# Value biases written into PSUM by ScalarE, low parts read from PSUM by VectorE, final normalisation on GpSimd

## The reference

```python
def layer(h, params):                      # second network, two layers
    u = einsum('bid,bjd->bij', h, h) / sqrt(D)
    a = softmax(u, axis=-1)
    delta = a * adjacency_matrix
    attn = delta / (sum(delta, axis=-1, keepdims=True) + 1e-10)
    hl = h @ wl.T + b_l
    hs = h @ ws.T + b_s
    hr = h @ wr.T + b_r
    ctx = (attn * upper) @ hl + diag(attn)[..., None] * hs + (attn * lower) @ hr
    o = (ctx - mean(ctx)) / sqrt(var(ctx) + 1e-12) * g + beta
    return relu(o)
...
x = layernorm(x + first_network(x, adj))
x = layernorm(x + second_network(x, adj))
```

## Time and profile before

| what | us |
|---|---|
| median of 3 runs | 1744.8 (1744.64 to 1747.77) |
| the profiled execution | 1744.34 |
| its span, first to last instruction | 1742.2 |
| TensorE busy | 1676.6 |
| VectorE, ScalarE, GpSimd busy | 1286.0, 884.4, 824.6 |
| TensorE's mean granted clock | 0.991 of full |

### The profile page before, as it was taken

One profiled execution on the slowest core, in us unless ns is written; L12 is line 12 of the kernel. 1 busy time (PEld: TensorE's weight loads), 2 busy tenths in 40 slices (PEclk: granted clock), 3 DMA queues, 4 the chain that ended last, 5 costly groups with the idle time before them and its releaser, 6 DMA issues.

```text
span 1742.2 us, 30190 instructions
## 1 busy us (share of the span) xinstructions
PE 1676.6 (96%) x9664; PEld 1581.4 (91%) x9664; DVE 1286.0 (74%) x2783; ACT 884.4 (51%) x1785; POOL 824.6 (47%) x860
## 2 busy tenths in 40 slices
PE   7999999999999999999999999999999999999994
PEld 6989989888988989989899999999999999999994
DVE  4587685967868587786877868678686786867866
ACT  4545455464554545455454545545455454544542
POOL 5143242423324243244466646567375663656635
PEclk9999999999999999999999999999999999999997
DMA  7015021020300202031131220303103021030201
GB/s 226 1 31 154 6 82 38 24 90 6 114 6 24 92 29 90 6 87 45 50 85 24 71 44 22 93 0 80 35 21 93 0 81 34 21 93 0 76 1 36
DMA packets 107991, 92.00 MB, mean 53 GB/s; under 512 B 63280, under 2 KB 101168, under 8 KB 107952
## 3 DMA queue, kind: packets, MB, share of 16 engines
q1 hardware_dynamic: 107952, 91.51, 18.3%
HBM read 66.33 MB, written 25.17 MB: 53 GB/s over the span
## 4 chain that ended last, share of the span: by engine, by line
issue 46%; POOL 27%; PE 19%; DVE 5%; ACT 2%; SPq 1%; POOLq 1%; DMA 0%; DVEq 0%; ACTq 0%
PE b_work L1153 11%; POOL s_v_lo L1347 8%; POOL g_qv_lo L622 3%; POOL b_ht L602 3%; POOL b_z L1371 3%; PE b_work L372 2%; POOL b_z L1373 2%; PE b_work L1165 2%; POOL s_expo L1358 1%; POOL s_keep L1341 1%; POOL s_rstd L1362 1%; PE b_score_ps L386 1%; PE b_work L396 1%; POOL g_keep_l L617 1%; POOL g_sigma L631 1%
## 5 line engine op out<-in xcount | busy, mean ns | idle before, releaser
L1153 PE MATMUL b_work<-b_w_hi,b_ht 128*128 128x384 f32 x2304 | 605.4, 337 | 2.4 <-DVE b_z L1500 1.7
L1153 PEld LDWEIGHTS b_work<-b_w_hi,b_ht 128*128 128x128 f32 x2304 | 418.0, 188 | 3.6 <-DVE b_z L1500 2.6
L1153 PE MATMUL b_work<-b_w_lo,b_ht 128*128 128x384 f32 x1152 | 385.3, 334 | 0.0
L372 PE MATMUL b_work<-b_ht,b_w_hi 128*128 128x512 f32 x1152 | 357.4, 391 | 9.8 <-DVE b_w_lo L697 9.8
L1347 POOL TENSOR_TENSOR s_v_lo<-s_v_full,s_v_hi 128x384 fp32r<-128x384 f32 x256 | 245.7, 978 | 197.4 <-ACT s_v_hi L1250 196.6
L622 POOL TENSOR_TENSOR g_qv_lo<-g_v_full,g_qv_hi 128x384 fp32r<-128x384 f32 x128 | 132.6, 1055 | 363.7 <-ACT g_qv_hi L495 363.7
L372 PEld LDWEIGHTS b_work<-b_ht,b_w_hi 128*128 128x128 f32 x1152 | 216.1, 189 | 51.4 <-issue 9.8
L372 PE MATMUL b_work<-b_ht,b_w_lo 128*128 128x512 f32 x576 | 225.8, 392 | 0.0
L1153 PEld LDWEIGHTS b_work<-b_w_lo,b_ht 128*128 128x128 f32 x1152 | 216.7, 188 | 0.0
L729 DVE TENSOR_TENSOR g_qv_lo<-b_work,g_qv_hi 128x512 fp32r<-128x512 f32 x192 | 128.7, 686 | 112.0 <-ACT g_qv_hi L483 110.2
L396 PE MATMUL b_work<-b_w_hi,b_ht 128*128 128x384 f32 x768 | 206.2, 336 | 0.0
(11 more groups left out here) (137 smaller groups left out, 3226.4 us busy)
## 6 DMA issues: line engine op xcount, KB each, us to landing
b_x_in<-in_x_t SPq DMA_DIRECT2D x16, 768.0 KB, 7.0
g_x_res<-in_x SPq DMA_DIRECT2D x16, 768.0 KB, 7.6
x<-b_z SPq DMA_DIRECT2D x16, 768.0 KB, 3.8
b_x_in<-x SPq DMA_DIRECT2D x64, 192.0 KB, 6.8
s_x_res<-x SPq DMA_DIRECT2D x16, 768.0 KB, 7.0
out<-b_z SPq DMA_DIRECT2D x15, 768.0 KB, 4.1
b_a_tr<-in_adj_t SPq DMA_DIRECT2D x64, 64.0 KB, 3.4
g_a_nat<-in_adj SPq DMA_DIRECT2D x32, 64.0 KB, 2.4
```

The lines of the kernel that those rows point to most:

```text
L372: mm = pe.matmul(bank[:], w, h, start=(n == 0), stop=(n == len(pairs) - 1))
L1153: mm = pe.matmul(bank[:, 0:H], h, w, start=(n == 0), stop=(n == len(pairs) - 1))
```

## The change

ScalarE writes ("seeds") the bias of a value job of side 0 or 1 into its bank before TensorE starts, and TensorE adds its nine products to it. ScalarE then copies the high part out of the bank, VectorE subtracts it from the bank and writes the low part, which frees the bank. `v_full` and GpSimd's `values_lo` are gone, and a value job of side 0 or 1 waits for its seed (`seeded`) in place of the free bank. The four final normalisations per unit move from ScalarE to GpSimd, except in the last pass. ScalarE's order within a unit is written anew; VectorE makes the probabilities ahead of jobs 3 to 5. At the hand-over VectorE's flips and low parts come earlier and the residual later, ScalarE's third `next_turn_out` comes earlier, two memsets move from GpSimd to VectorE, GpSimd's masks of stream 1 go ahead of its weight parts, and SyncE's first store goes ahead of two weight loads.

The diff, cut to its core:

```diff
@@ gated network, ScalarE, last unit
                     next_turn_out(0)
                     next_turn_out(1)
+                    next_turn_out(2)
                 exponentials(i, unit)
...
-                if not more:
-                    next_turn_out(2)
@@ gated network, VectorE, query parts of the last unit
                             query_lo(i, unit + 1, j)
+                            if last and unit == UNITS - 2 and j == QB - 2:
+                                next_flip(0)
+                                next_flip(1)
@@ gated network, VectorE, up_to_contexts
-                if s is not None:
+                if s is not None and more:
                     add_residual(i, s)
...
                 if not more:
-                    next_flip(0)
-                    next_flip(1)
-                mask_scores(i, unit)
-                if not more:
                     next_turn_lo(0)
                     next_flip(2)
+                    next_turn_lo(1)
+                    next_turn_lo(2)
+                mask_scores(i, unit)
                 biased_value(i, unit, 1)
...
                 biased_value(i, unit, 3, uses=1 if more else 2)
+                if not more:
+                    add_residual(i, s)
@@ SyncE
             sp.wait_ge(folded, 1)
+            store_last(0)
             load_weight(0)
             load_weight(1)
-            store_last(0)
@@ TensorE, values
-                bank = work_bank(i, unit, j)
+                if side < 2:
+                    pe.wait_ge(seeded, nth(i, unit, 2 * NT, 2 * t + side))
+                    bank = work[(unit * WN + j) % RING]
+                else:
+                    bank = work_bank(i, unit, j)
...
-                    mm = pe.matmul(bank[:, 0:H], h, w, start=(n == 0), stop=(n == len(pairs) - 1))
+                    mm = pe.matmul(bank[:, 0:H], h, w, start=(n == 0 and side == 2), stop=(n == len(pairs) - 1),
+                                   skip_group_check=True)
@@ TensorE, contexts
-                    pe.wait_ge(v_lo_ready, nth(i, unit, 2 * NT, 2 * t + 1))
+                    pe.wait_ge(work_free, freed(i, unit, t * SIDES + 1))
@@ ScalarE
-            def values_hi(i, unit, t):
...
+            def seed(i, unit, j):
+                t, side = value_job(j)
+                act.wait_ge(work_free, freed(i, unit, j - RING))
+                nc.scalar.activation(work[(unit * WN + j) % RING][:, 0:H], bias[:, side, layer_of(unit), :], ACT.Copy)\
+                    .then_inc(seeded, 1)
+
+            def value_hi(i, unit, j):
+                t, side = value_job(j)
+                act.wait_ge(work_full, nth(i, unit, WN, j))
+                nc.scalar.activation(v_hi[:, t, side, 0:H], work[(unit * WN + j) % RING][:, 0:H], ACT.Copy)\
+                    .then_inc(v_hi_ready, 1)
...
             def first_half(i, unit):
+                seed(i, unit, 0)
+                seed(i, unit, 1)
                 exponentials(i, unit)
-                values_hi(i, unit, 0)
+                seed(i, unit, 3)
+                value_hi(i, unit, 0)
+                value_hi(i, unit, 1)
+                seed(i, unit, 4)
             def second_half(i, unit, more, tail):
-                values_hi(i, unit, 1)
...
                 probabilities_hi(i, unit)
+                value_hi(i, unit, 6)
+                seed(i, unit, 9)
+                if flip_next:
+                    turn_out(i, unit + 1, 0)
+                value_hi(i, unit, 7)
+                seed(i, unit, 10)
+                if flip_next:
+                    turn_out(i, unit + 1, 1)
                 if tail:
                     gated_normalise(1)
-                flip_next = more and layer_of(unit + 1) == 0
-                if flip_next:
+                if turn_next:
                     turn_out(i, unit + 1, 0)
                     turn_out(i, unit + 1, 1)
-                values_hi(i, unit, 2)
+                value_hi(i, unit, 9)
                 if more:
-                    for k in range(2 if flip_next else 0, KO):
-                        turn_out(i, unit + 1, k)
-                values_hi(i, unit, 3)
+                    turn_out(i, unit + 1, 2)
+                value_hi(i, unit, 10)
@@ ScalarE, one_pass
                         first_half(i, unit + 1)
-                    normalise(i, unit, more)
-                    if more:
+                        seed(i, unit + 1, 6)
+                        normalise(i, unit, (0, 1))
+                        value_hi(i, unit + 1, 3)
+                        normalise(i, unit, (2, 3))
+                        value_hi(i, unit + 1, 4)
+                        seed(i, unit + 1, 7)
                         second_half(i, unit + 1, not (last and unit == UNITS - 2), first and unit == 0)
...
-                    if unit >= STREAMS:
+                    if last and unit >= STREAMS:
                         final_normalise(i, unit - STREAMS, tiles=NT if more else NT // 2)
@@ ScalarE, first unit: exponentials, seed 3, high parts of probabilities, then
+            value_hi(0, 0, 0)
+            value_hi(0, 0, 1)
+            seed(0, 0, 4)
+            seed(0, 0, 6)
             gated_normalise(0)
-            values_hi(0, 0, 0)
-            values_hi(0, 0, 1)
+            value_hi(0, 0, 3)
+            value_hi(0, 0, 4)
+            seed(0, 0, 7)
             weight_hi(0)
+            value_hi(0, 0, 6)
+            seed(0, 0, 9)
@@ GpSimd
+            def final_normalise(s):
+                for t in range(NT):
+                    nc.gpsimd.tensor_scalar(z[s][:, t, 0:H], z[s][:, t, 0:H], frstd[s][:, t:t + 1],
+                                            foffset[s][:, t:t + 1], ALU.mult, ALU.add).then_inc(out_ready, 1)
...
                     roots(i, unit)
-                    if more:
-                        values_lo(i, unit + 1, 0)
...
+                    if unit == 0 and not first:
+                        final_normalise(1)
+                    if unit == UNITS - 1 and not last:
+                        final_normalise(0)
@@ VectorE, biased_value
                 if side < 2:
...
+                    dve.wait_ge(v_hi_ready, nth(i, unit, 2 * NT, 2 * t + side))
+                    nc.vector.tensor_tensor(v_lo[:, t, side, 0:H], bank[:, 0:H], v_hi[:, t, side, 0:H].bitcast(F32),
+                                            ALU.subtract).then_inc(work_free, 1)
@@ VectorE, up_to_contexts
+                probabilities(i, unit)
                 for j in range(3, 6):
                     biased_value(i, unit, j)
...
-                probabilities(i, unit)
+                probabilities_lo(i, unit)
                 biased_value(i, unit, 6)
-                probabilities_lo(i, unit)
```

More of the change, by code:

```diff
@@ L949, in softmax_layers @@
     LAST_GT = 1
-    VF = 4
     HALF = P // 2
@@ L1257, in final_normalise, with normalise @@
                                          bias=foffset[s][:, t:t + 1]).then_inc(out_ready, 1)
-            def normalise(i, unit, more):
+            def normalise(i, unit, tiles):
                 layer, s = divmod(unit, STREAMS)
                 act.wait_ge(offset_ready, nth(i, unit, 1, 0))
-                for t in range(NT if layer == 0 or more else LAST_GT):
+                for t in tiles:
                     nc.scalar.activation(z[s][:, t, 0:H], z[s][:, t, 0:H], ACT.Identity, scale=rstd[:, t:t + 1],
@@ L1646, in _ @@
             nc.vector.memset(v_own[:, :, H:H + 1], 1.0)
+            nc.vector.memset(v_hi[:, :, :, H:HC].bitcast(F32), 1.0)
+            nc.vector.memset(v_lo[:, :, :, H:HC].bitcast(F32), 0.0)
             biased_value(0, 0, 3)
```

60 lines of the change are left out of this document (21 added, 39 removed).

## The result

The changed kernel takes 1732.74 us (median of 4 runs, 1731.75 to 1733.57) against 1745.92 us of the kernel before, run beside it: ratio 0.9919, 95% interval 0.9907 to 0.9931. Profiled execution to profiled execution it is 1731.75 against 1744.34 us, span 1730.2 against 1742.2: -12.0 us of span where the sum said -18.0. Faster, as forecast, and 5.7 us above the predicted 1727.

The account below looks back on a forecast made before the run. TensorE, busy for 96% of the span, was taken to bound the kernel. Terms -15.4 - 4.5 + 0.4 + 1.5 = -18.0 us against 1744.34 gave 1726.3, for the median 1727; range 1716 to 1738.

Parts of the forecast that it names:

- (1): Contexts of the unit after the fourth, seven passes: TensorE's paired waits on GpSimd's low parts go, -15.4 us.
- (2): TensorE's slow stretches that begin near those waits: with the waits gone the clock drops go, -4.5 us.
- (3): Middle of all units: ScalarE's added seeds and high-part copies from PSUM fit without delaying TensorE, 0 us.
- (4): At 14 unit boundaries: job 0 also waits for a seed, but VectorE comes earlier; net +0.4 us.
- (7): Tail behind the last matmul: it keeps its instructions, 0 us.
- (5): Final normalisation moved to GpSimd: about 1.0 us a tile, taken up by slack in its queue, 0 us.
- (6): Hand-over to the second network: earlier start, then waits on late seeds and weights; net +1.5 us.
- Late boundary: Unit boundaries: GpSimd's normalisation takes 1.96 us a tile, seven waits partly return, 9 us, 1736 us; chance 0.14.

Follow-up runs that it names:

- the kernel with the forty memsets: Changed kernel plus 40 one-column memsets in front of VectorE's program, their tile allocated behind all others: 1724.79 us, ratio 0.9884.

## Why the prediction was right, and where it was off

The direction was right, and the waits and slow stretches that were to go went. Two signs named for it did not come: passes take 106.65 us and not 105.9, and outside the first unit TensorE waits 1.04 to 1.20 us for a seed once per pass, where well under 0.3 was said. The median lies 0.7 us above the forecast's own band of 1722 to 1732.

(1) **The pairs.** Right, and mis-sized to the bad side. No wait on GpSimd is left in the contexts. But they cost more than the 15.4 us of the list. From the contexts' first matmul to the next fold that unit took 6.90 to 6.97 us in the passes without a clock drop, and takes 4.25 now: 2.7 us a pass, 18.8 in seven. In the kernel before, the last matmul ahead of the longer wait is this, and the next, the first of the earlier trace rows, starts 2.04 us after it where 0.18 is usual:

```profile
1198.29 0.34 PE L1165 MATMUL b_work<-s_v_hi,s_prob_lo 128*128 128x386 f32 x1
```

The list shows 1.71 us of that.

(2) **The clock.** Right. The passes at 0.98 are at 1.00, and no TensorE wait of 1.7 us stands ahead of them: 109.73 + 109.68 + 109.45 less three times 108.1 is -4.6 us, against -4.5. The new wait of 1.04 to 1.20 us leaves the clock at 1.00.

(3) **The middle of a unit.** Right, nearly to the figure. Lines by cost, changed kernel (busy, mean ns | idle before):

```profile
L1492 DVE TENSOR_TENSOR s_v_lo<-b_work,s_v_hi 128x384 fp32r<-128x384 f32 x256 | 139.3, 554 | 108.4 <-ACT s_v_hi L1260 107.5
...
L1254 ACT ACTIVATE b_work<-b_bias 128x384 f32<-128x384 f32 x256 | 126.4, 494 | 128.9 <-DVE b_z L1530 82.0 <-DVE s_v_lo L1492 24.8 <-DVE s_v_own L1496 19.2
...
L1412 POOL TENSOR_SCALAR b_z<-b_z,s_frstd,s_foffset 128x384 f32<-128x384 f32 x56 | 36.4, 666 | 0.1
```

The seed took 494 ns (0.53 us taken). In the kernel with the forty memsets the cover, from seed's end to first matmul, is 0.31 us at job 3 of second-layer units (0.24 worked out), 0.70 at job 4 and 0.99 at job 7 (0.6 each). The doubled seeds show that there was no more than that. In the changed kernel itself job 3 of the fourth unit lost this cover to the idle time before L1482, and 0.22 us in each of six passes.

(4) **The unit boundary.** Mis-sized, to the bad side. I took +0.4 us. From the first matmul of the fold to job 0, the first unit took 1.05 to 1.09 us in the third to the eighth pass before and takes 0.63 now; the second unit took 0.63 (more only in slow stretches) and takes 0.73. Together that is -2.0 us. VectorE came through the residuals early enough that the first unit's seed is done 0.10 us ahead of job 0. In the second unit job 0 starts 0.05 us behind its seed, which is 0.1 us late. With the back edge repaired, the second to the last pass together are 25.7 us shorter than before (the second 2.7, the loop 19.8, the last 3.2): pairs 18.8, clock 4.6, boundaries 2.0, and 0.3 at the end, see (7).

(5) **The final normalisation.** Its cost of 0 held, at 666 ns a tile where I took 1.0 us. One tile as input took 666 ns, a multiplication of two 947 ns. The Trainium skill, GPSIMD Engine Reference, section 4.1 Engine selection, has one-input work there at roughly line-rate and two-input work about twice as slow as on VectorE. The second agrees, with 947 ns against the 0.51 us of a residual beside an idle GpSimd. The first agrees in direction only: VectorE does the same normalisation of a tile in the last pass (L1599) in 478 ns, and 666 is 1.4 times that. What the step lacked is its other half. The move is not a neutral exchange; with the seeds in place, the old place in ScalarE's order costs 125 us.

(6) **The hand-over.** Mis-sized: +1.5 us summed, -3.75 + 9.13 = +5.4 measured. The mechanisms were the named ones, late seeds at jobs 7 (2.06 us, 2.5 forecast) and 9 (3.19, 1 to 3) and the late weight copy; of the 1.0 us forecast at jobs 4 and 6 only some 0.2 came. The step that failed is the start. Job 0 was put at 848.2 and began at 850.98, because its bank waits for statistics behind four residuals (VectorE, changed kernel):

```profile
843.80 4.74 DVE L803 SCALAR_TENSOR_TENSOR b_z<-b_z,g_x_res 128x384 f32<-128x384 f32 x4
848.47 1.47 DVE L808 BATCH_NORM_STATS2 g_fstats<-b_z 128x6 f32<-128x384 f32 x3
849.85 0.55 DVE L761 BATCH_NORM_STATS2 g_stats<-b_work 128x6 f32<-128x384 f32 x1
```

They took 1.19 us each on the average, beside GpSimd's low parts and masks. At 0.51 each, the price beside an idle GpSimd, the seed would have been done at 848.3, which is the 848.2 of the forecast. The prediction does not show its price there; this is the one that fits, and the price beside a busy GpSimd, 1.02, stood in the earlier trace rows. Everything behind it is then 2.8 to 3.6 us later than forecast: seed 6 at 861.5 (858.7), the copy at 870.6 (867). The run with earlier statistics shows that a timely start alone would not have helped: the next bound, at job 4, is VectorE's own chain.

(7) **The tail.** 0 forecast; the last unit with the tail is 0.3 us shorter.

**What the sum did not have.** The loop's code: +8.1 us in five passes (533.36 against 525.2 with the memsets), 1.36 a pass at job 4 of the second unit and 0.22 at job 3 of the fourth, and +0.2 in the second pass, where only the latter comes. Measured, then: -18.8 - 4.6 - 2.0 + 5.4 - 0.3 + 8.3 = -12.0, the whole of the difference. Errors of 4 us (hand-over) and 8 (code) to the slow side stand against 3.4 (pairs) and 2.4 (boundary) to the fast side. They cancel only in part, and a third of the forecast 18.0 us is missing; that the time was missed by only 0.3% is luck as much as sizing. "Late boundary" would have given the time better and for a reason that is not there.

## What to carry to other kernels

Take a step off a loaded engine only with the step that makes room where it goes, and look at what a moved instruction waits for, not at its length: the same normalisations cost nothing or 125 us, by whether something urgent stands behind them. In an in-order queue put work that is ready ahead of work that waits; that alone was 4.7 us. Size what a wait costs by the starts of the instructions around it and not by the list: two listed waits of 1.71 and 0.47 us cost 2.7, one of 1.04 cost 1.36. And when the size of a loop's code changes, look at its back edge in the order of time: an idle time that ends on "issue", with packets on the instruction queue in each pass, was cured here by moving where the code begins.

## What the runs showed of the hardware

The code of a loop can be fetched anew in each pass. VectorE's loop has 316 instructions (323 before), counted with its semaphore and register instructions; fetches of 8192 bytes follow at a distance of 129 counted instructions. Where the start lay 19 instructions ahead of such a point, as worked out from the counts, the first block was gone at the back edge and VectorE stood still for 2.2 to 2.3 us, in five passes of five. With 40 more in front it never did, with 110 more it did, and the kernel before did with 80 more; the loop of 387 instructions did too. In the changed kernel the stop ended 1.9 to 2.0 us after a fetch had started. That it is the number of blocks that the loop touches (four, not three) is an inference: it forecast the three padded positions, but the kernel before starts within 3 instructions of a block's edge by these counts, too near to be told, and the buffer itself was not measured.

Moving the tiles' addresses by 160 bytes a partition made each pass of the first network 0.4 us longer (104.4 against 104.04 us with the same instructions and the tile last). With 440 bytes it was 0.9 us longer, and with 320 bytes, in the kernel before, 0.9 to 1.0 in five passes and 0.3 to 0.4 in two; these two runs also had more instructions in front and no counterpart with the tile last. Which tile it is stays open.
